# Two attention layers of one program: first query stacks laid without DRAM, projections in idle banks, the start of each layer in another order

## The reference

```python
# 16 heads of 8 channels; layer 0 turns q and k by position (rope), layer 1 doesn't
q = layernorm(x) @ Wq + bq;  k = ctx @ Wk + bk;  v = ctx @ Wv + bv
p = softmax(q @ k.T / sqrt(8))              # per head and sequence
x = x + tanh(g) * ((p @ v) @ Wo + bo)
```

## Time and profile before

| what | us |
|---|---|
| median of three runs (lowest, highest) | 1623.83 (1617.97, 1623.98) |
| the profiled execution | 1621.11 |
| its span | 1619.3 |
| PE busy in the span | 1384.8 |
| DVE, ACT, POOL busy | 861.7, 547.1, 418.2 |

### The profile page before, as it was taken

The page is one execution under the profiler, slowest core; times in us unless marked ns, Lnnn a source line. Parts: engine busy times, 40 slices in busy tenths (PEclk is TensorE's granted clock), DMA queues, the critical chain, the costliest instruction groups (busy, mean ns, idle before and its releaser), DMA issues. The chain is left out here.

```text
span 1619.3 us, 26329 instructions
## 1 busy us (share of the span) xinstructions
PE 1384.8 (86%) x8869; PEld 865.7 (53%) x8869; DVE 861.7 (53%) x2507; ACT 547.1 (34%) x1291; POOL 418.2 (26%) x729
## 2 busy tenths in 40 slices
PE   5799886995999859896994994756999999999998
PEld 2577663543787636555883773543444444344343
DVE  5577646874676523323663433754455546446425
ACT  2366555652577622223551331430101011011001
POOL 3687501104777100001344123620000000000000
PEclk9699987995799979995776997887999999999999
DMA  6766730004677468000001111232211302202200
GB/s 181 169 153 150 161 83 1 1 1 106 157 170 178 84 244 354 0 1 27 27 27 36 49 55 43 65 117 105 105 51 61 111 19 93 112 1 110 105 7 13
DMA packets 74720, 143.01 MB, mean 88 GB/s; under 512 B 13430, under 2 KB 53878, under 8 KB 64742
## 3 DMA queue, kind: packets, MB, share of 16 engines
q1 hardware_dynamic: 68038, 133.89, 28.4%
q0 software_dynamic: 3296, 6.76, 1.4%
q10 hardware_dynamic: 3264, 0.79, 0.3%
HBM read 99.33 MB, written 41.09 MB: 87 GB/s over the span
## 5 line engine op out<-in xcount | busy, mean ns | idle before, releaser
L2700 DVE TENSOR_TENSOR l3f_weighted_T<-l3f_w_e,l3f_xnT 128x512 f32<-128x512 f32 x128 | 88.4, 691 | 129.7 <-PE psum L2451 114.5
L2451 PE MATMUL psum<-l3f_weighted_T,w_l3f_q 128*128 128x512 f32 x256 | 133.7, 604 | 16.5 <-DVE l3f_weighted_T L2700 14.7
L2451 PE MATMUL psum<-l3f_weighted_T,w_l3f_k 128*128 128x512 f32 x256 | 131.6, 596 | 0.0
L2451 PE MATMUL psum<-l3f_weighted_T,w_l3f_v 128*128 128x512 f32 x256 | 131.3, 594 | 0.0
L2460 PE MATMUL psum<-l3f_weighted_T,w_l3f_o 128*128 128x512 f32 x256 | 124.3, 624 | 1.7 <-DVE l3f_weighted_T L2700 1.7
L2700 DVE TENSOR_TENSOR l3f_weighted_T<-l3f_w_e,l3f_oT 128x512 f32<-128x512 f32 x128 | 88.4, 692 | 57.2 <-PE psum L2460 30.3
L707 DVE TENSOR_REDUCE l1x_minus_max<-psum 128x4 f32<-128x512 f32 x128 | 84.7, 686 | 61.4 <-PE psum L360 60.5
L707 DVE TENSOR_REDUCE l0x_minus_max<-psum 128x4 f32<-128x512 f32 x128 | 84.4, 686 | 38.6 <-PE psum L360 37.9
L111 POOL TENSOR_TENSOR l3f_ln_rstd<-l3f_ln_mean_var,eps 128x4 f32<-128x4 f32 x8 | 2.0, 245 | 355.8 <-DVE l3f_ln_mean_var L104 355.8
L2460 PEld LDWEIGHTS psum<-l3f_weighted_T,w_l3f_o 128*128 128x128 f32 x256 | 39.3, 188 | 82.8 <-DVE l3f_weighted_T L2700 78.1
L2451 PEld LDWEIGHTS psum<-l3f_weighted_T,w_l3f_v 128*128 128x128 f32 x256 | 48.9, 191 | 61.8 <-issue 61.8
(11 more groups left out here) (486 smaller groups left out, 2991.5 us busy)
## 6 DMA issues: line engine op xcount, KB each, us to landing
l3f_w_e<-l3f_weights_scratch SPq DMA_DIRECT2D x32, 1024.0 KB, 4.7
sorted_x<-zeros SPq DMA_DIRECT2D x1, 16896.0 KB, 59.5
l0x_k_stack<-l0x_k_scratch SPq DMA_DIRECT2D x48, 192.0 KB
l0x_q_stack<-l0x_q_scratch SPq DMA_DIRECT2D x48, 192.0 KB
l1x_k_stack<-l1x_k_scratch SPq DMA_DIRECT2D x48, 192.0 KB
l1x_q_stack<-l1x_q_scratch SPq DMA_DIRECT2D x48, 192.0 KB
w_l2f_w<-in_l2f_w SPq DMA_DIRECT2D x2, 2048.0 KB, 13.2
l0x_k_scratch<-l0x_k_parts SPq DMA_DIRECT2D x16, 192.0 KB, 6.4
```

What stands on the lines that cost most here:

```text
L2451: ins = pe.matmul(bank[:, :], w[name][:, e, :], xe[:, e % 2, :], start=(e == 0), stop=(e == NE3 - 1))
L2700: dve.tensor_tensor(xe[:, e % 2, :], wE[:, g % 2, e, :], src, ALU.mult).then_inc(s_xe, 1)
```

## The change

In both layers:
- the first half of the q stacks of groups 0 and 1 doesn't go through DRAM: nine DMAs of 8 partitions x 16 heads x 256 tokens (64 KB) copy each part from SBUF to its three places in the stack (`lay_straight`), each issued when its part is split. On SP's queue they stand behind the k loads;
- `banks_of` and `xn_bank` give k of group 1, q of group 1, v of group 0 and the turned x of groups 0 and 1 banks that are idle then;
- the statistics of group 1 come before `rotate k(0)` on DVE, POOL's order is changed, and PE's prologue is written in another order;
- scores 0 to 3 run with only `turn_max(0)` between them; `project_k(2)` follows; `turn_max(1)`, `turn_xn(2)`, `turn_max(2)`, `project_q(2)` go into loop step 0.

In layer 1 PE begins with `keep_busy(2)`: two matmuls whose product nobody reads. In layer 0, x and ctx come in eight pieces, not four, the later ones loaded inside the loop over groups.

```diff
+        def banks_of(n, g):
+            return {("k", 1): bankS, ("q", 1): bankT, ("v", 0): bankT}.get((n, g), [bankP0, bankP1])
+        def xn_bank(g):
+            return bankA if g < 2 else bankP1
...
+            def lay_straight(g):
+                for a in range(NPART):
+                    if a < NPART - 1:
+                        links = 4 if rope else 3
+                        sp.wait_ge(s_first if g == 0 else s_split, links + (2 if rope else 1) + 2 * a)
+                    else:
+                        sp.wait_ge(s_parts["q"], g + 1)
+                    for b in range(NPART):
+                        at = (b * NPART + (a - b) % NPART) * HD
+                        sp.dma_start(stack["q"][at:at + HD, g, 0, :, :], parts["q"][:, a, half(0)])\
+                          .then_inc(s_stack["q"][g][0], 16)
...
             load("k", 0, 1)
-            store("q", 0)
-            load("q", 0, 0)
+            lay_straight(0)
+            store("q", 0, (1,))
             load("q", 0, 1)
...
+            def keep_busy(n):
+                for _ in range(n):
+                    pe.matmul(bankA[:, :], v1[:, 0, 0, 0:HEADS - 1, :].rearrange("p h d -> p (h d)")[:, 0:P],
+                              v1[:, 0, :, :, :].rearrange("p c h d -> p (c h d)")[:, 0:T], start=True, stop=True)
...
+            if not rope:
+                pe.wait_ge(s_fill, 4)
+                keep_busy(2)
+            k.wait_weights(pe, name)
+            pe.wait_ge(s_fill, 4)
+            project_k(0)
+            if not rope:
+                project_k(1)
+                project_v(0)
+            turn_xn(0)
+            if rope:
+                project_v(0)
+            project_q(0)
+            turn_xn(1)
+            if rope:
+                project_k(1)
+            project_q(1)
+            project_v(1)
...
+            turn_max(0)
...
+            project_k(2)
+            pe.wait_ge(s_out["q"], 2)
...
             unit(3)
             if 1 <= j <= NSEQ:
                 turn(j - 1)
+            if j == 0:
+                turn_max(2)
             if j + LEAD - 1 < NSEQ:
                 turn_max(j + LEAD - 1)
+            if j == 0:
+                project_q(2)
             if c == 0 and t + 2 < NG:
                 project_v(t + 2)
...
             pool.wait_ge(s_fill, 4)
-            for g in range(3):
-                moments(g)
+            moments(0)
+            moments(1)
             split("k", 1)
+            moments(2)
+            split_max(0)
             split("q", 1)
-            split_max(0)
             split_max(1)
-            moments(3)
             split_max(2)
             split("k", 2)
+            moments(3)
...
             moments(0)
+            moments(1)
             rotate("k", 0)
             split_first("k")
-            moments(1)
```

More of the change, by code:

```diff
@@ L256, in heads_attention, with straight @@
         stores = {"k": 1, "q": 2}
+        def straight(n, g, hf):
+            return n == "q" and g < 2 and hf == 0
         def stack_landed(eng, n, g, hf):
-            eng.wait_ge(s_stack[n][g % 2][hf], 16 * loads[n] * (g // 2 + 1))
+            loaded = loads[n] * (g // 2 + 1)
+            if n == "q" and hf == 0:
+                loaded += NPART * NPART - loads["q"]
+            eng.wait_ge(s_stack[n][g % 2][hf], 16 * loaded)
         def parts_stored(eng, n, g, hf):
-            eng.wait_ge(s_stored[n][hf], 16 * stores[n] * (g + 1))
+            if straight(n, g, hf):
+                stack_landed(eng, n, g, hf)
+            else:
+                through = g + 1 if n == "k" or hf == 1 else g - 1
+                eng.wait_ge(s_stored[n][hf], 16 * stores[n] * through)
         block = ctx.enter_context(nc.Block())
@@ L303, in _ @@
                 k.load_x(sp, 3)
-                k.load_ctx(sp, 3)
             for g in range(1, NG):
                 store("k", g)
-                store("q", g)
-                load("k", g, 0)
-                load("q", g, 0)
+                if g == 1:
+                    load("k", g, 0)
+                    lay_straight(g)
+                    store("q", g, (1,))
+                else:
+                    store("q", g)
+                    load("k", g, 0)
+                    load("q", g, 0)
+                if name == "l0x" and g + 2 < NG:
+                    k.load_ctx(sp, g + 2)
+                if name == "l0x" and g + 3 < NG:
+                    k.load_x(sp, g + 3)
                 load("k", g, 1)
@@ L416, in out @@
                 pe.matmul(bankM[:, P:2 * P], aT[:, j % 2, :], w["wo"][:, :], start=True, stop=True).then_inc(s_o, 1)
[L418 to L434, removed]
+            if not rope:
[16 more added lines that the diff above has]
+            project_v(1)
+            pe.matmul(bankM[:, 0:P], bcast(w["bv"][:, 0:1], [P, P]), w["wo"][:, :], start=True, stop=True).then_inc(s_bp, 1)
+            pe.wait_ge(s_out["k"], 2)
+            for u in range(4):
+                scores(0, u)
+            for u in range(4):
+                scores(1, u)
+            turn_max(0)
+            for u in range(4):
+                scores(2, u)
+            for u in range(4):
+                scores(3, u)
+            project_k(2)
+            pe.wait_ge(s_out["q"], 2)
             pe.wait_ge(s_ones, 16)
-            pe.wait_ge(s_fill, 4)
             for j in range(NSEQ + 2):
@@ L448, in _ @@
                 unit(1)
+                if j == 0:
+                    turn_max(1)
                 if j >= 2:
@@ L2791, in __init__ @@
         self.ctxT = sb("ctxT", [P, NSEQ * P], F32)
-        self.s_x = [ctx.enter_context(nc.semaphore(f"x_in_{i}")) for i in range(4)]
-        self.s_ctx = [ctx.enter_context(nc.semaphore(f"ctxT_in_{i}")) for i in range(4)]
+        self.s_x = [ctx.enter_context(nc.semaphore(f"x_in_{i}")) for i in range(NG)]
+        self.s_ctx = [ctx.enter_context(nc.semaphore(f"ctxT_in_{i}")) for i in range(NG)]
         self.constants = sb("constants", [P, width(CONSTANTS)], F32)
@@ L2936, in _ @@
                 for piece in (1, 2):
+                    k.load_x(sp, piece)
                     k.load_ctx(sp, piece)
[L2938 removed]
             @block.vector
```

103 lines of the change are left out of this document (63 added, 40 removed).

## The result

The changed kernel is slower: median 1648.2 us (1643.52 to 1655.48, four runs) against 1623.9; ratio 1.0162, interval 1.0117 to 1.0208. Six more executions of it gave 1.0177 (1.0129 to 1.0226). That is 26 and 29 us, by the intervals 19 to 37; the forecast was 16, with 1650 (a ratio of 1.0161) as the upper end.

A forecast was written before the change was run, and what follows sets the result against it. PE was taken to bound both main loops, so prologue shifts pass to the end: 1621.11 + 5.1 (layer 0) + 13.3 (layer 1) = 1639.5, stated as 1640 us, range 1612 to 1650.

The forecast's parts named there:

- the marks: Each layer's first scores and second turned scores; the latter forecast 5.1 us later in layer 0, 13.3 in layer 1.
- The copies: Before the first scores: nine narrow copies take 9.1 us behind the k loads, putting layer 0's first scores at 38.0.
- partitions: Reason for the copies' price: the partitions reached set the rate, eight giving 61 to 69 GB/s.
- the walk: The prediction's step-by-step timing of both layers' prologues, from the start to the second turned scores; +5.1 and +13.3 us.
- Layer 0 behind the first scores: From layer 0's first scores at 38.0 to the second turned scores at 72.7, against 67.63 before.
- POOL's chain: Layer 0, behind the first scores: maxima, group 2's keys, splits, statistics and add_bias take 27.55 us, `turn_max(3)` at 65.55.
- `keep_busy` +5.1: Layer 1's start: two dummy matmuls delay the first projection's evacuation from 377.14 to 382.2, with nothing covering it.
- +13.3: Layer 1: second turned scores at about 436, against 422.70 before.
- POOL's chain of 23.65: Layer 1, behind first scores at 406.0: the same chain with shorter split and projection gives 429.7.
- the queue's 431.2: Layer 1: group 1's stores, loads and nine copies in the DMA queue end later than POOL's chain, at 431.2.
- The clock rival: Prologues: PE's clock goes to full, halving projections; 1632 with slow copies (chance 0.10), 1618 with fast ones (0.15).
- a shift of their start passes to the end nearly whole: Main loops of layers 0 and 1: PE-bound, so prologue delays of 5.1 and 13.3 us reach the total nearly whole.

The follow-up runs named there:

- e5_twoq: Changed kernel with four of group 0's nine straight copies issued from ACT's queue; one run, 1637.79 us.
- e9_order: Changed kernel with the work between first scores and main loop in the order of before; ratio to before 1.007.
- e1_dram: Changed kernel with the first halves of groups 0 and 1's q stacks stored to DRAM and loaded as before; ratio to before 1.0105.
- e2_nobusy: Changed kernel without the two dummy matmuls at the start of layer 1; ratio to before 1.0119.
- a0_again: The changed kernel itself, unedited, executed again; ratio to before 1.0177.
- e10_all: Changed kernel with order, copies, dummies, x and ctx pieces, and layer 1's early statistics and early fill wait undone; ratio to before 0.9998.
- e7_l1new: Changed kernel with only layer 1 changed; layer 0 and the loads of x and ctx as before; ratio to before 1.0102.
- e8_l0new: Changed kernel with only layer 0 changed; layer 1 as before; ratio to before 1.008.
- e6_fillwait: Changed kernel with five more dummy matmuls in loop step 0, ahead of the scores of sequence 4; ratio to before 1.0171.

## Why the prediction was right or wrong

The direction and the sum of the marks held; the size of the whole was too small (16 us, against 26 and 29), and the measured ratio lies at and just above the range's end.

- **The copies**: nine in 9.1 us and first scores at 38.0; measured 38.4, and 35.7 to 38.4 over the profiles with copies. At the 62 to 75 GB/s of most of them nine take 8 to 9.5 us (an estimate), so the price was right; its reason (partitions) is what `e5_twoq` speaks against. That the first scores came out is in part luck: the walk has 37.2 without the copies (36.2 and 0.95 for the statistics), but through DRAM the new prologue has 34.2 to 35.1. So the copies cost 2.6 us there, not 1; and the 36.2 of before was 34.5 in another execution of the same layer 0.
- **Layer 0 behind the first scores**: 34.7 us; measured 35.9, but not for the walk's reason alone. The walk let POOL's chain set `turn_max(3)`, at 65.55, and left out the copies of group 1, which the first scores of that group want in layer 0 too. PE stood 8.80 us for that stack, until 62.73, with the turned maxima behind it; POOL's chain ended at 66.50, `turn_max(3)` came at 67.76. Two chains ended close together, so the number came right without the wait. `e9_order` shows that it is the order which makes the wait costly; through DRAM (`e1_dram`) it is still 6.8 us.
- **Layer 1**: `keep_busy` +5.1; measured 3.8 at the evacuation in the first profile and 4.9 in the second, 3.1 and 4.2 at k's loads. The clock rose at different times. Without the dummies the early statistics and the early wait for the fills have k's loads 2.1 later than before (`e2_nobusy`), a cost that the walk had for layer 0 alone; so the dummies' own part is 1 to 2. The forecast's +13.3 at the second turned scores was 11.7, and 14.5 at `a0_again`'s mark (62.1 less 47.6). POOL's chain of 23.65 is 24.4 by the terms that the walk names; the queue's 431.2 is later either way.
- **The clock rival**: full clock did come at layer 1's start, in the first profile for what follows the dummies, in the second only for what follows the first projection, and gave back a part of the dummies' own delay at most.
- **POOL's order**: not costed at all. On `e10_all` it was worth 3.3 us at mark 1. In the changed kernel POOL idles 8.6 us at that place, but its copies stand behind other transfers on SP's queue, so what it costs there was not tried.
- **The base**: the 18.4 us were added to the profiled execution, which was 2.7 us below the median that the result is compared with. On the median the sum is 1642, and the end of its range 1653.
- **The step that failed**, as far as is known, is the first part's "a shift of their start passes to the end nearly whole", with +5.1 and +13.3 as all that the change costs. The marks shift by 18 to 19 us against the profile of before, by 22 to 23 against the unchanged layers of `e7_l1new` and `e8_l0new`; the median by 26 and 29 (19 to 37). What makes the rest stays open, and it isn't clear of the noise. In the first profile it stands in the main loops, but over the profiles it doesn't: layer 0's loop takes 164.3 to 179.0 us, 169.4 on the average, in the seven profiles that keep layer 0's order and copies, and 166.8 and 170.4 unchanged; layer 1's takes 143.8 to 159.9, 152.8 on the average, in the six that keep layer 1's order, copies and dummies, and 150.4 and 153.8 unchanged. A loop's length goes with its mean clock (0.99 at 143.8 us, 0.92 at 159.8). Whether the late start lowers it more often isn't shown; `e6_fillwait` raised the clock for some 6 us, and not in the steps behind them. And layer 0's +5.1 was itself small: its marks come 5 to 10 us later.

## What to carry to other kernels

An engine takes its program in order, so work that is ready must not stand behind a wait for something late: moving work of group 2 and two turned maxima behind the scores of sequence 4 cost some 10 us of 1622, the largest part here by its median. Before a copy is narrowed to save a round trip, compare bytes over its own rate with what the round trip takes. And when the walk fits the marks, take the marks of before, too, from more than one execution, and check what lies behind them before calling the shift whole.

## What the runs showed of the hardware that was not expected

Copies of 64 KB from 128 partitions into eight, one behind the other, ran at 62 to 75 GB/s in six profiles and at 88 in `e9_order`, at a DMA share of 0.62 to 0.66 in all, and a second queue didn't help. Behind the same two dummy matmuls TensorE's granted clock rose ahead of the first projection in one execution of the changed kernel (1.88 us for two projections) and inside the second one in another (3.17 us). The kernel before, unchanged, took 1607.9 to 1638.7 us in one set of 29 runs. The same loop of the same kernel took 159.1 and 143.8 us in two profiled executions, with TensorE's mean granted clock at 0.92 and 0.99.
